# Four adjacent rows of a batch in one partition, and the first rows loaded as two transfers of two tiles

## The chip, the cores and the metric

The kernel runs on one core of a Trainium2 chip. The metric is the device time of one execution in microseconds (us); lower is better. Inputs lie in DRAM (HBM) when it starts and the result must lie there when it ends.

## The reference

A gated block of a Flamingo-like network, all in float32: a LayerNorm, an attention whose keys and values are 512 context rows followed by the 512 rows themselves, and a feed-forward part with the signs of its weights. There are 4 batches of 512 rows and 512 features.

```python
def reference(x, ctx, mask, g_xattn, g_ffn, wq, wk, wv, wo, up_w, down_w, up_scale, down_scale, output_scale):
    n = layernorm(x)                                   # x is (4, 512, 512), rows of 512 features
    q, k_new, v_new = n @ wq.T, n @ wk.T, n @ wv.T
    k, v = concat([ctx, k_new], 1), concat([ctx, v_new], 1)      # 1024 keys
    x = x + tanh(g_xattn) * (softmax(q @ k.T / sqrt(512)) @ v @ wo.T)
    h = relu((layernorm(x) @ sign(up_w).T) * up_scale)            # 2048 hidden
    return x + tanh(g_ffn) * (h @ sign(down_w).T) * down_scale * output_scale
```

Each output row depends on its own input row and, through the softmax, on all rows of its batch in any order: if the rows of a batch are numbered differently inside the kernel, the new keys and values are numbered in the same way, and the result is the same once each row is stored where it belongs.

## The kernel before

All four batches of `x` live in one tile, `rows`, of 128 partitions x 16 tiles x 512 features (a *tile* is here 128 rows of a batch, one in each partition). Tile `r` of a batch holds rows 128r to 128r+127: partition p has row 128r + p (`x_v`, L51, and `out_v`, L54). So the load of one tile reads 256 KB that lie together in DRAM, 2 KB for each partition, and the load of a whole batch reads four pieces of 2 KB for each partition.

Every float32 product is made of three matmuls over a high and a low part (`PASSES`), so each operand goes through ACT (a copy to the high part, rounded) and then DVE or POOL (the low part, the difference). Engines are driven by instruction lists written out by hand, and each waits on semaphores.

*SP* issues all the transfers, in the order of its list (L160 to L211). At the start it issues the first batch's tiles 0 and 1 of `x`, each a transfer with its own semaphore `x0_in[r]` (L170), then the first two quarters of `wk` (L172), then tiles 2 and 3, then the other two quarters of `wk`, then `wq` (L173), the first context (L174), `wo`, `wv`, three gates, two scale vectors and the first signs. A quarter of `wk` is 2 KB out of every 8 KB in DRAM, for `wk` is laid out as `[p, e, c, n]` and quarter `e` is loaded for all p. After that SP waits for POOL's low parts of `wk` (`w_ready`) and loads the whole of batch 1 of `x` (L186) into the place of `wk`'s raw rows, and later batches 2 and 3 (L188, L192) in the same way. At the end it stores the 16 result tiles of 256 KB (L204, and L210 for the last four), each when its rows are ready.

*DVE* starts with `first_stats(0)`, `first_stats(1)`, `first_norm(0)`, `first_norm(1)`, `first_stats(2)`, then the low parts of the turned tiles 0 and 1 (L626), `first_stats(3)`, the low parts of the first two quarters of `wk` (L730), `first_norm(2)` and `first_norm(3)` (L725), and the low parts of turned tiles 2 and 3. `first_stats(r)` waits for `x0_in[r]` (L716) and computes mean and variance (L717, L719, L721); POOL turns variance to the inverse standard deviation (`rstd`, L232) in between. Later batches are normed from L656 on.

*ACT* starts with the high parts of `wk`'s quarters 0 and 1 (L484), the high parts of turned tiles 0 and 1 (L492), `wk`'s quarters 2 and 3, and turned tiles 2 and 3.

*PE* starts with the transposes of normed tiles 0 and 1 (L281, into `turn`), then `first_k_half` (L392), matmuls of 256 columns: for output chunks 0 and 1 of K the pass high x high over the first 256 rows (8 matmuls, which need both turned tiles' high parts), the pass with the low part of the rows (8, which need `turn_lo` at 2), the pass with the low part of `wk` (8, `first_lo`), 16 matmuls for chunks 2 and 3; then the transposes of tiles 2 and 3 (L281, into `proj`), 8 matmuls that need POOL's low parts of `wk` (L237), and 48 for the second 256 rows, which need the turned tiles 2 and 3. From then on PE has Q, the scores, and all the rest (L289, L440, L453).

Of the kernel before, what the change touches and what calls it, by code (L numbers as in the profile page):

```python
# [11 lines left out]
P = 128  # L12
# [4 lines left out]
def gated_block(nc, x, ctx_kv, ctx_turned, g_xattn, g_ffn, wk, wq, wv, wo, ffn_w, up_scale, down_scale,  # L17
# [3 lines left out]
    BATCH, ROWS, DIM = x.shape  # L21
    HC = ffn_w.shape[0]
    RT = ROWS // P
# [24 lines left out]
        return PROJS_FIRST + PROJS_BATCH * b  # L48

    row_tiles = "(r p) d -> p r d"  # L50
    x_v = x.rearrange("b (r p) d -> b p r d", p=P)  # L51
    ctx_v = ctx_kv.rearrange("b (r p) d -> b p r d", p=P)
    ctx_turned_v = ctx_turned.rearrange("b (c p) k -> b p c k", p=P)
    out_v = out.rearrange("b (r p) d -> p (b r) d", p=P)  # L54

    with ExitStack() as stack:
        def sb(name, shape, dt=F32):
            return stack.enter_context(nc.sbuf_tensor(name, shape, dt))
# [4 lines left out]
        def sem(name):  # L63
            return stack.enter_context(nc.semaphore(name))

        rows = sb("rows", [P, BATCH * RT, DIM])
# [49 lines left out]
            return wide(n) if n < DC else proj[:, n % 2, :]  # L116

        small_in, ctx_in, out_stored = map(sem, ("small_in", "ctx_in", "out_stored"))
        x0_in = [sem(f"x0_in{i}") for i in range(RT)]
        x_in = {b: sem(f"x_in{b}") for b in range(1, BATCH)}  # L120
        wk_in = [sem(f"wk_in{i}") for i in range(DC)]
        w_in = {w: sem(f"w_in{w}") for w in (W_Q, W_V, W_O)}
# [18 lines left out]
        LAST = RT * (BATCH - 1)  # L141
# [10 lines left out]
        def turned_split(b):  # L152
            return 2 * b

        def values_split(b):
            return 2 * b + 1
# [3 lines left out]
        @block.sync  # L160
        def _(sp):
            def load_signs(j):
                if j >= 1:
                    sp.wait_ge(signs_ready, j)
                sp.dma_start(raw_w[:, :, :], ffn_w[j]).then_inc(signs_in, 16)


            for half in ((0, 1), (2, 3)):
                for r in half:
                    sp.dma_start(rows[:, r, :], x_v[0, :, r, :]).then_inc(x0_in[r], 16)  # L170
                for e in half:
                    sp.dma_start(raw_of[W_K][:, e, :], wk[:, e].rearrange("p c n -> p (c n)")).then_inc(wk_in[e], 16)  # L172
            sp.dma_start(raw_of[W_Q], wq.rearrange("p e c n -> p e (c n)")).then_inc(w_in[W_Q], 16)  # L173
            sp.dma_start(raw_ctx[:, :, :], ctx_turned_v[0]).then_inc(ctx_in, 16)  # L174
            sp.dma_start(raw_of[W_O], wo.rearrange(row_tiles, p=P)).then_inc(w_in[W_O], 16)
            sp.dma_start(raw_of[W_V], wv.rearrange(row_tiles, p=P)).then_inc(w_in[W_V], 16)
            for i, g in enumerate((g_xattn, g_ffn, output_scale)):
                sp.dma_start(gates_raw[:, i:i + 1], g.rearrange("(a n) -> a n", a=1).broadcast_to([P, 1])
                             ).then_inc(small_in, 16)
            sp.dma_start(out_gain[:, :], down_scale.rearrange("(a n) -> a n", a=1).broadcast_to([P, DIM])  # L180
                         ).then_inc(small_in, 16)
            sp.dma_start(hid_gain[:, :], up_scale).then_inc(small_in, 16)
            load_signs(0)

            sp.wait_ge(w_ready, SPLIT[W_K] + DC - BY_VECTOR)
            sp.dma_start(rows[:, RT:2 * RT, :], x_v[1]).then_inc(x_in[1], 16)  # L186
            sp.wait_ge(w_ready, SPLIT[W_Q] + DC - BY_VECTOR)
            sp.dma_start(rows[:, 2 * RT:3 * RT, :], x_v[2]).then_inc(x_in[2], 16)  # L188
            sp.wait_ge(ctx_ready, turned_split(0) + 1)
            sp.dma_start(raw_ctx[:, :, :], ctx_v[0]).then_inc(ctx_in, 16)  # L190
            sp.wait_ge(w_ready, SPLIT[W_V] + DC - BY_VECTOR)
            sp.dma_start(rows[:, 3 * RT:4 * RT, :], x_v[3]).then_inc(x_in[3], 16)  # L192

            for b in range(1, BATCH):
                sp.wait_ge(ctx_ready, values_split(b - 1) + 1)
                sp.dma_start(raw_ctx[:, :, :], ctx_turned_v[b]).then_inc(ctx_in, 16)
                sp.wait_ge(ctx_ready, turned_split(b) + 1)
                sp.dma_start(raw_ctx[:, :, :], ctx_v[b]).then_inc(ctx_in, 16)

            for j in range(1, HC):  # L200
                load_signs(j)
            for t in range(BATCH * RT - RT):
                sp.wait_ge(out_ready, t + 1)
                sp.dma_start(out_v[:, t, :], rows[:, t, :]).then_inc(out_stored, 16)  # L204
            for r in (0, 2, LAST_POOL, 3):
                if r == LAST_POOL:
                    sp.wait_ge(pool_out_ready, 1)
                else:
                    sp.wait_ge(out_ready, RT * (BATCH - 1) + LAST_DVE.index(r) + 1)
                sp.dma_start(out_v[:, LAST + r, :], rows[:, LAST + r, :]).then_inc(out_stored, 16)  # L210
            sp.wait_ge(out_stored, 16 * BATCH * RT)  # L211

        @block.gpsimd
# [406 lines left out]
        def _(dve):  # L620
# [92 lines left out]
                    proj_out(m + 12 + e, chunk(qT, e), SCALE)  # L713

            def first_stats(r):
                dve.wait_ge(x0_in[r], 16)  # L716
                dve.bn_stats(stats[:, r, :], rows[:, r, :]).then_inc(stats_done, 1)  # L717
                dve.wait_ge(stats_done, r + 1)
                dve.bn_aggr(mean_var[:, r, :], stats[:, r, :]).then_inc(meanvar_done, 1)  # L719
                dve.wait_ge(meanvar_done, r + 1)  # L720
                dve.tensor_scalar(var_eps[:, r:r + 1], mean_var[:, r, 1:2], EPS, None, ALU.add).then_inc(eps_done, 1)  # L721
# [6 lines left out]
            def first_weight_low(e):  # L728
                dve.wait_ge(w_hi, SPLIT[W_K] + e + 1)
                dve.tensor_tensor(weights[:, W_K, LO, e, :], raw_of[W_K][:, e, :],  # L730
                                  weights[:, W_K, HI, e, :].bitcast(F32), ALU.subtract).then_inc(first_lo, 1)

            first_stats(0)
            first_stats(1)
            first_norm(0)
            first_norm(1)
            first_stats(2)
            turn_out(0, part(xT, 0))
            turn_out(1, part(xT, 1))
# [123 lines left out]
```

## Time and profile before

| | us |
|---|---|
| median of 3 runs | 629.65 |
| lowest, highest | 629.64, 630.89 |
| the profiled execution | 629.46 |
| its span in the trace | 627.4 |
| PE busy | 615.0 (98% of the span) |
| DVE, ACT, POOL busy | 247.9, 177.6, 71.1 |
| granted PE clock, mean | 0.999 |

The time of the profiled execution is 2.06 us more than its span: that lies outside of what the trace has. In the trace an instruction is given by its start in us from the span's start, its duration, engine, line, and what it writes and reads; square brackets say how long its engine had been idle before it and who ended that. PEld is the loading of weights into PE, beside the matmuls. SPq is SP's issuing of a transfer, not the transfer; the time from an issue to the landing is given separately. A matmul's own duration overlaps with its neighbours', so a stretch of matmuls is priced by its length over its count.

### The profile page before, as it was taken

How to read it: one execution, taken by the hardware profiler on the slowest of the kernel's cores; microseconds unless marked ns; L12 is line 12 of the kernel's file. 1: busy time of each engine (PE TensorE's matmuls, PEld its weight loads, DVE VectorE, ACT ScalarE, POOL GpSimd, SP SyncE). 2: the span in 40 equal slices, each digit the busy share in tenths (PEclk: the TensorE clock that was granted, in tenths of full speed). 3: DMA queues.
4: the chain of work that ended last, by engine and by line, in shares of the span. 5: the costliest groups of instructions: out<-in, count | busy, mean ns of one | idle time of the engine just before them, and what ended most of it. 6: DMA issues, size and time to landing. Idle time of an engine off the chain costs nothing.

```text
span 627.4 us, 6781 instructions
## 1 busy us (share of the span) xinstructions
PE 615.0 (98%) x2864; PEld 512.5 (82%) x2864; DVE 247.9 (40%) x430; ACT 177.6 (28%) x273; POOL 71.1 (11%) x49
## 2 busy tenths in 40 slices
PE   5999999999999999999999999999999999999997
PEld 5888888888888888888888888888888888888885
DVE  5336322226322226222236223453574366436234
ACT  3624321214221224231236243322212222312211
POOL 3660202000202001202001100100010001000002
PEclk9999999999999999999999999999999999999999
DMA  8740102000101000102013323200010010001001
GB/s 301 282 139 1 68 0 68 0 1 1 67 1 67 1 0 1 68 0 68 0 34 101 100 70 132 68 0 1 18 50 1 0 47 21 1 1 67 2 0 67
DMA packets 13517, 30.05 MB, mean 48 GB/s; under 512 B 1456, under 2 KB 1456, under 8 KB 13360
## 3 DMA queue, kind: packets, MB, share of 16 engines
q1 hardware_dynamic: 13488, 29.64, 13.5%
q8 instruction: 22, 0.36, 0.2%
q14 instruction: 7, 0.06, 0.0%
HBM read 25.44 MB, written 4.19 MB: 47 GB/s over the span
## 4 chain that ended last, share of the span: by engine, by line
PE 96%; ACT 1%; DVE 1%; DMA 1%; SPq 0%; issue 0%; ACTq 0%
PE proj L289 32%; PE score L289 21%; PE proj L440 19%; PE score L453 18%; PE turn L281 4%; PE score L392 2%; DMA rows<-in_wk 1%; ACT four_x L488 0%; DVE rows L812 0%; ACT four_x L492 0%; DVE raw_ctx L809 0%; DVE four_x L626 0%; DVE neg_max L646 0%; ACT probs L500 0%; ACT probsT L492 0%; ACT weights L509 0%
## 5 line engine op out<-in xcount | busy, mean ns | idle before, releaser
L440 PE MATMUL proj<-four_x,weights 128*128 128x512 f32 x512 | 127.6, 392 | 0.0
L453 PE MATMUL score<-weights,probsT 128*128 128x512 f32 x512 | 126.5, 390 | 0.2 <-DVE probsT L769 0.2
L453 PEld LDWEIGHTS score<-weights,probsT 128*128 128x128 f32 x512 | 96.1, 188 | 20.6 <-DVE probsT L769 0.6
L440 PEld LDWEIGHTS proj<-four_x,weights 128*128 128x128 f32 x512 | 95.3, 188 | 19.3
L289 PE MATMUL score<-four_x 128*128 128x512 f32 x384 | 89.9, 392 | 0.0
L289 PE MATMUL proj<-probsT,four_x 128*128 128x512 f32 x384 | 89.9, 392 | 0.0
L599 ACT ACTIVATE probs<-proj,hid_gain 128x512 f32<-128x512 f32 x64 | 43.9, 687 | 147.6 <-PE proj L440 147.6
L496 ACT ACTIVATE four_x<-proj 128x512 fp32r<-128x512 f32 x60 | 35.8, 599 | 172.6 <-PE proj L289 172.6
L289 PEld LDWEIGHTS proj<-probsT,four_x 128*128 128x128 f32 x384 | 71.5, 188 | 14.5
L289 PEld LDWEIGHTS score<-four_x 128*128 128x128 f32 x384 | 71.5, 188 | 14.5
L632 DVE TENSOR_TENSOR four_x<-proj,four_x 128x512 fp32r<-128x512 f32 x44 | 30.3, 691 | 122.1 <-ACT four_x L496 122.1
L289 PE MATMUL proj<-four_x,weights 128*128 128x512 f32 x336 | 76.8, 389 | 0.0
L289 PEld LDWEIGHTS proj<-four_x,weights 128*128 128x128 f32 x336 | 63.0, 188 | 13.0
L767 DVE CAST probsT<-probs 128x512 fp32r<-128x512 f32 x64 | 27.2, 425 | 111.6 <-ACT probs L599 111.6
L242 POOL TENSOR_TENSOR four_x<-raw_ctx,four_x 128x2048 fp32r<-128x2048 f32 x8 | 36.9, 4610 | 122.0 <-ACT four_x L488 122.0
L289 PE MATMUL proj<-weights,four_x 128*128 128x512 f32 x192 | 45.8, 394 | 0.3 <-DVE four_x L632 0.3
L769 DVE TENSOR_TENSOR probsT<-probs,probsT 128x512 fp32r<-128x512 f32 x64 | 44.3, 692 | 2.2
L289 PE MATMUL score<-weights,four_x 128*128 128x512 f32 x192 | 44.2, 389 | 0.0
L289 PEld LDWEIGHTS score<-weights,four_x 128*128 128x128 f32 x192 | 36.1, 188 | 7.5
L289 PEld LDWEIGHTS proj<-weights,four_x 128*128 128x128 f32 x192 | 35.5, 188 | 7.6 <-DVE four_x L632 0.5
L500 ACT ACTIVATE probs<-score,neg_max 128x1024 f32<-128x1024 f32 x16 | 17.9, 1117 | 71.8 <-DVE neg_max L646 71.8
L225 POOL TENSOR_TENSOR var_eps<-mean_var,eps 128x4 f32<-128x4 f32 x7 | 1.7, 237 | 318.4 <-DVE mean_var L661 318.4
(59 smaller groups left out, 367.2 us busy)
## 6 DMA issues: line engine op xcount, KB each, us to landing
raw_w<-in_ffn_w SPq DMA_DIRECT2D x16, 512.0 KB, 3.3
raw_ctx<-in_ctx_turned SPq DMA_DIRECT2D x4, 1024.0 KB, 5.4
raw_ctx<-in_ctx SPq DMA_DIRECT2D x4, 1024.0 KB, 5.2
result<-rows SPq DMA_DIRECT2D x16, 256.0 KB, 2.0
rows<-in_x SPq DMA_DIRECT2D x3, 1024.0 KB, 6.7
rows<-in_x SPq DMA_DIRECT2D x4, 256.0 KB, 4.2
rows<-in_wk SPq DMA_DIRECT2D x4, 256.0 KB, 5.5
rows<-in_wq SPq DMA_DIRECT2D x1, 1024.0 KB, 8.2
```

What stands on the lines that cost most here:

```text
L242: pool.tensor_tensor(ctx_side[:, LO], raw_ctx[:, :, :], ctx_side[:, HI].bitcast(F32), ALU.subtract).then_inc(ctx_ready, 1)
L281: last = pe.transpose(bank[:, k * P:(k + 1) * P], tile, ident[:, :])
L289: last = pe.matmul(bank, lhs(l), rhs(r), start=start and i == 0, stop=stop and i == 2)
L392: last = pe.matmul(proj_bank(e)[:, cut], weights[:, W_K, l, e, c * P:(c + 1) * P], xT[:, r, c, cut], start=i == 0 and c == 0, stop=i == 2 ...
L440: last = pe.matmul(proj[:, j % 2, :], signs[:, j, 0, k * P:(k + 1) * P], four_x[:, c, s, k, :], start=(k == 0 and s == HI), stop=(k == DC ...
L453: last = pe.matmul(wide(r), hid_split[:, j % HR, s, r * P:(r + 1) * P], signs[:, j, 1, :], start=(j == 0 and s == HI), stop=(j == HC - 1 a ...
L496: act.activation(dst, proj_bank(n), ACT.Copy, scale=scale).then_inc(proj_hi, 1)
L500: act.activation(probs[:, t % 2, :], score[t % 2][:, :, :].rearrange("p a n -> p (a n)"), ACT.Exp, bias=neg_max[:, t:t + 1], accum_out=row ...
L599: act.activation(hid[:, j % HR, :], proj[:, j % 2, :], ACT.Relu, scale=hid_gain[:, j:j + 1]).then_inc(relu_done, 1)
L632: dve.tensor_tensor(dst(LO), proj_bank(n), dst(HI).bitcast(F32), ALU.subtract).then_inc(proj_lo, 1)
L767: dve.tensor_copy(slot[:, HI, :], hid[:, j % HR, :]).then_inc(hid_hi, 1)
L769: dve.tensor_tensor(slot[:, LO, :], hid[:, j % HR, :], slot[:, HI, :].bitcast(F32), ALU.subtract).then_inc(hid_ready, 1)
```

## The change

The rows of a batch are dealt out otherwise: partition p holds rows 4p to 4p+3, and tile `r` has row 4p + r in partition p. The view of `x` and that of the result change in the same way, so each row is stored where it came from. A partition's four rows are now 8 KB that lie together in DRAM.

The first batch's rows are loaded by two transfers instead of four: one for tiles 0 and 1, one for tiles 2 and 3, each 4 KB for each partition out of every 8 KB. Each has one semaphore, so there are two `x0_in` instead of four, and `first_stats(r)` waits for `x0_in[r // 2]`. The loads of batches 1 to 3 keep their place and size, but read 8 KB in one piece for each partition instead of four of 2 KB. The 16 stores keep their place, size and semaphores, but write 2 KB out of every 8 KB instead of 256 KB together. No instruction of PE, ACT, DVE or POOL is added, removed or moved.

```diff
     row_tiles = "(r p) d -> p r d"
-    x_v = x.rearrange("b (r p) d -> b p r d", p=P)
+    x_v = x.rearrange("b (p r) d -> b p r d", r=RT)
...
-    out_v = out.rearrange("b (r p) d -> p (b r) d", p=P)
+    out_v = out.rearrange("b (p r) d -> b p r d", r=RT)
...
-        x0_in = [sem(f"x0_in{i}") for i in range(RT)]
+        x0_in = [sem(f"x0_in{i}") for i in range(RT // 2)]
...
             for half in ((0, 1), (2, 3)):
-                for r in half:
-                    sp.dma_start(rows[:, r, :], x_v[0, :, r, :]).then_inc(x0_in[r], 16)
+                sp.dma_start(rows[:, half[0]:half[1] + 1, :], x_v[0, :, half[0]:half[1] + 1, :]
+                             ).then_inc(x0_in[half[0] // 2], 16)
                 for e in half:
                     sp.dma_start(raw_of[W_K][:, e, :], wk[:, e].rearrange("p c n -> p (c n)")).then_inc(wk_in[e], 16)
...
-                sp.dma_start(out_v[:, t, :], rows[:, t, :]).then_inc(out_stored, 16)
+                sp.dma_start(out_v[t // RT, :, t % RT, :], rows[:, t, :]).then_inc(out_stored, 16)
...
-                sp.dma_start(out_v[:, LAST + r, :], rows[:, LAST + r, :]).then_inc(out_stored, 16)
+                sp.dma_start(out_v[BATCH - 1, :, r, :], rows[:, LAST + r, :]).then_inc(out_stored, 16)
...
             def first_stats(r):
-                dve.wait_ge(x0_in[r], 16)
+                dve.wait_ge(x0_in[r // 2], 16)
```

## Rows read from the trace of the kernel before

**Rows 1.** The page: busy time by engine; the transfers of the result.
```profile
PE 615.0 (98%) x2864; PEld 512.5 (82%) x2864; DVE 247.9 (40%) x430; ACT 177.6 (28%) x273; POOL 71.1 (11%) x49
...
result<-rows SPq DMA_DIRECT2D x16, 256.0 KB, 2.0
```
**Rows 2.** Waits of PE: line waited for, us in total, times, longest us.
```profile
PE turn L281 <- DVE normed L725: 6.2, 1, 6.2
PE score L392 <- ACT four_x L492: 0.8, 1, 0.8
PE score L392 <- DVE four_x L626: 0.6, 1, 0.6
```
**Rows 3.** The chain that ended last, 0 to 30 us: start, us, what.
```profile
2.11 5.27 DMA rows<-in_wk
...
8.04 0.98 ACT four_x L492 x2
...
9.06 7.47 PE score L392 x40
...
18.97 6.02 PE score L392 x48
```
**Rows 4.** Timeline of 0 to 22 us: start, duration, engine, line, operation.
```profile
0.74 0.86 SPq L170 DMA_DIRECT2D rows<-in_x  x2
...
3.54 0.70 DVE L717 BATCH_NORM_STATS2 stats<-rows 128x6 f32<-128x512 f32 x1 [3.54 <-DMA rows<-in_x]
...
6.25 2.03 PE L281 MATMUL turn<-ident,normed 128*128 128x128 f32 x8 [6.25 <-DVE normed L725]
6.53 0.63 ACT L484 ACTIVATE weights<-rows 128x512 fp32r<-128x512 f32 x1 [4.51 <-DMA rows<-in_wk]
6.55 0.55 DVE L725 TENSOR_SCALAR normed<-rows,mean_var,rstd 128x512 f32<-128x512 f32 x1 [0.45 <-POOL rstd L232]
...
7.94 1.06 ACT L492 ACTIVATE four_x<-turn 128x512 fp32r<-128x512 f32 x2
8.05 0.69 DVE L717 BATCH_NORM_STATS2 stats<-rows 128x6 f32<-128x512 f32 x1 [0.95 <-DMA rows<-in_x]
...
9.07 1.28 DVE L626 TENSOR_TENSOR four_x<-turn,four_x 128x512 fp32r<-128x512 f32 x2
...
11.27 1.28 DVE L730 TENSOR_TENSOR weights<-rows,weights 128x512 fp32r<-128x512 f32 x2
...
13.63 2.54 POOL L237 TENSOR_TENSOR weights<-rows,weights 128x512 fp32r<-128x512 f32 x2 [1.12 <-DVE normed L725]
...
16.37 0.60 SPq L186 DMA_DIRECT2D rows<-in_x  x1
17.00 1.08 ACT L492 ACTIVATE four_x<-proj 128x512 fp32r<-128x512 f32 x2 [6.34 <-PE proj L281]
17.13 1.01 PEld L392 LDWEIGHTS score<-four_x,weights 128*128 128x128 f32 x8
```
**Rows 5.** Issue to landing: tiles 0 and 1; `wk` quarter 0; tiles 2 and 3.
```profile
DMA to landing us min/median/max: 2.8/2.9/3.0
...
DMA to landing us min/median/max: 4.9/4.9/4.9
...
DMA to landing us min/median/max: 5.4/5.5/5.6
```
**Rows 6.** GB/s in 40 slices of 0.125 us, 0 to 5, then 5 to 10.
```profile
GB/s 0 0 0 0 0 0 0 0 0 0 0 0 0 0 16 115 98 16 131 229 360 410 410 410 377 426 410 410 361 344 295 246 246 197 279 328 262 197 82 49
...
GB/s 49 98 131 213 213 230 229 229 262 279 262 279 344 279 377 393 377 377 393 377 361 410 295 393 311 426 393 426 410 442 492 393 377 426 410 541 475 262 393 524
```
**Rows 7.** Busy time by stretch; after POOL: granted clock, DMA share, GB/s.
```profile
9.00:14.50 5.50, 5.44 (x25) 5.44 (x26) 4.48 (x10) 1.27 (x3) 1.96 (x2) 1.00 1.02 400
```
**Rows 8.** Batch 1: landing of its load (L186), first use.
```profile
DMA to landing us min/median/max: 12.4/12.4/12.4
...
51.02 2.46 DVE L656 BATCH_NORM_STATS2 stats<-rows 128x6 f32<-128x512 f32 x4
```
**Rows 9.** The last two stores: issue to landing.
```profile
DMA to landing us min/median/max: 2.0/2.1/2.1
```

## The prediction, made before the changed kernel was run

> **What bounds the kernel now.** I read the page's busy times first, then the waits of PE, then the chain that ended last, then the timeline of the first 22 us, and last the rates and landings of the transfers. PE is busy for 615.0 of 627.4 us [rows 1]. Of its waits only three matter, and all three lie in the first 19 us: 6.2 us until the first normed tile, 0.8 us for ACT's copies, 0.6 us for DVE's low parts [rows 2]. The rest of the span is a row of matmuls without a gap worth naming, and then a tail of some us with the last sums and stores. So a load that is off the path by many us can't matter, and the change can move the time in two places alone: in what stands ahead of PE's start, and in the last store.
>
> The chain of the start [rows 3] goes by a quarter of `wk` that lands at 7.38, ACT's copies that end at 9.02, and PE's 40 matmuls from 9.06. It doesn't name `x`. The reader must see how near the other branch runs. Tile 0 is issued at 0.74 and DVE starts on it at 3.54; the second normed tile ends at 6.55 + 0.55 = 7.10; PE's eight transposes end at 6.25 + 2.03 = 8.28; ACT's second copy starts at about 7.94 + 1.06 - 0.58 = 8.42 [rows 4]. The branch of `x` has only 8.42 - 8.28 = 0.14 us to spare.
>
> **The change part by part.**
>
> *The first pair.* Before, tile 0 lands 2.8 us after its issue, at 3.54; tile 1, issued 0.43 us later at 1.17, lands 3.0 us after that, at 4.17 [rows 4, 5]. The pair is now one transfer with one semaphore, issued at 0.74, and DVE can't start before all 512 KB are there. The transfers run at 410 GB/s in this stretch [rows 6], so 256 KB more cost 0.64 us: 3.54 + 0.64 = 4.18. Pieces of 4 KB instead of 2 KB may save a little: where `wq` comes in with pieces of 8 KB, from 8.5 us on, the rate has slices of 442 to 541 [rows 6], and at 442 the pair's 512 KB would take 0.09 us less. I take 4.10, so DVE starts 0.56 us later. Below, the bound is 3.9 us (the whole rate of the best slices, and one issue less in front); above, it is the landing of a strided read as in the first rival.
>
> *What that delays.* DVE's chain of the two tiles has no other outside wait than POOL's `rstd`, which moves with it. Its tile 1 was never late for it: it landed at 4.17 and DVE came to it about 1 us after 3.54. So the whole chain shifts by 0.56: the second normed tile ends at 7.66, the transposes at 8.84, ACT's second copy starts at 8.86 instead of 8.42, and PE's first matmul at 9.50 instead of 9.06: 0.44 us later. The two loads of `wk` get their issues 0.45 us earlier, but the bytes ahead of them on the queue are the same, and ACT isn't waiting for them any more.
>
> *What 0.44 us are worth at the end.* Between 9.06 and 14.5 PE makes 25 matmuls in 5.44 us, 0.218 us each [rows 7]; the 48 of the same shape later take 6.02 us, 0.125 each [rows 3]. That is the lower of the clock's two levels (256 columns at 1.2 GHz are 0.213 us), although the view prints a granted clock of 1.00 for the stretch: its record seems not to reach back so far, and the matmuls themselves are the better witness. The 40 matmuls of 7.47 us [rows 3] are then some 26 at the lower and 14 at the upper level, and the rise is near 14.7. If it stays there, a late start takes matmuls out of the slow stretch and puts them in the fast one: 0.44 x 0.125 / 0.218 = 0.25 us. If it moves with the start of the work, all 0.44 us are lost. I take 0.3, near the first, as I see no reason for the rise to move by so little a shift. On this the Trainium skill, page "TensorE: Matmul & The Clock Gate", Part 1, says that the default clock is the throttled one, that activity releases it, and that the point of the rise varies by about 500 ns from run to run because it isn't tied to the kernel's start; by that page the term could be 0.25 us with about 0.2 us either way, an estimate, and no view here can tell it from the other reading.
>
> *The second pair.* Tile 2 lands at 8.05, where DVE is waiting for it, and tile 3 at about 3.07 + 5.6 = 8.67 [rows 4, 5]. Now both land together at about 8.6. The wait stands in `first_stats(2)`; behind it on DVE are the low parts of the turned tiles 0 and 1, which PE's second eight matmuls need. They end at 9.07 + 1.28 = 10.35 now, and at 10.90 then. PE needs them after its first eight: at 9.50 + 8 x 0.218 = 11.24. That leaves 0.34 us where there are 0.45 now. Next: the low parts of `wk`, 11.27 to 12.55 now [rows 4], come 0.55 us later; the first is ready at 12.5 and wanted at 12.98, the second ready at 13.1 and wanted at 13.86. Then `normed` of tiles 2 and 3 and, behind them, POOL's low parts, which end at 13.63 + 2.54 = 16.17 now, 16.72 then; PE wants them at about 17.2 [rows 4] and later. Every one of these is covered, by 0.3 us at the least; if the pair lands later than 8.95 the first cover is gone, and from there on each 0.1 us costs up to 0.1 us. I put it at nothing, with 0 to 0.3 us as bounds.
>
> *The 0.6 us wait at 18.97* is for turned tiles 2 and 3, whose transposes stand behind the 40 matmuls on PE. It moves with them and stays as long as it is.
>
> *The loads of batches 1 to 3.* Batch 1 is issued at 16.37, behind POOL's low parts, and lands 12.4 us later, at 28.8; DVE first reads it at 51.02 [rows 4, 8]. Half a us later, or some tenths of a us shorter through the larger pieces, it is hidden by 22 us. Batches 2 and 3 have a whole batch more. Nothing. What stands behind them on SP's queue (contexts, signs) moves by half a us and is wanted far later.
>
> *The issues.* SP has two issues less of 0.43 us each, 0.86 for two [rows 4]. SP isn't on the path behind the first pair: what it issues then queues for the same engines. Nothing.
>
> *The stores.* Sixteen of 256 KB, 2.0 us each [rows 1]; twelve are covered by matmuls. The last lands about 2.0 us after its issue [rows 9], and that ends the span. It is still 128 pieces of 2 KB, but 8 KB apart in DRAM. No row shows such a write. The nearest are the reads of `wk` with the same spacing: quarters 2 and 3, from 8.2 us on, run in slices of 295 to 492 GB/s, as fast as anything [rows 6]; quarter 0 is slow, and belongs to the rival below. So nothing, with -0.1 to +0.5 us as bounds.
>
> The sum for the profiled execution: 629.46 + 0.3 = 629.76. The median of the runs shown lies 0.19 us above that execution, so the median of the changed kernel should be 629.95 us.
>
> **The rivals.**
>
> *A strided first read is slow (slower).* The first pair reads 4 KB out of every 8 KB over 1 MB, where a tile read 256 KB in one stretch. `wk`'s quarter 0 reads with just this spacing and is the first touch of its tensor: it lands at 1.65 + 4.9 = 6.55, which is 2.38 us after tile 1 for a quarter that is worth 0.64 at 410 GB/s, and the rate falls to 49 GB/s in between [rows 5, 6]. If the pair meets the same 1.7 us, it lands at 5.8, PE starts 2.26 - 0.14 = 2.12 us late, and the loss is 1.2 us (the rise stays) to 2.1 us (it moves): a median of 630.85 to 631.8, say 631.3. Against it speaks that tile 0, also a first touch, started with slices near 16 to 131 GB/s for half a us only, and that quarter 0 may have been slow for its place in time and not for its spacing: quarters 2 and 3 weren't. It decides for "slower" from a landing of the pair at about 5 to 6 us. The Trainium skill, page "DMA: Bandwidth & Descriptors", section "Latency and other measured facts", has a loss of rate for row pitches of 512 KiB and up; with our pitch of 8 KiB it would have this rival at nothing, and that no run here shows yet.
>
> *The clock rises later (slower).* Each us that the lower level lasts longer costs 1 - 0.125 / 0.218 = 0.43 us. The runs of before spread by 1.24 us, which would be a rise 2.9 us later. If the late start pushes the median of the new runs into that case, it is 629.95 + 1.24 = 631.2.
>
> *The start gets faster (below before).* If the larger pieces and the issue saved bring the pair in at 3.7 us and the second pair before 8.05, the shift of the branch is no more than its 0.14 us to spare, and ACT, no more held by a quarter of `wk` that was issued 0.45 us later, starts its copies some tenths earlier. That gives 629.4 to 629.6. For it speaks only the saved issue; against it, that the bytes come at the full rate already.
>
> *The change doesn't do what it says.* If the pair is cut into pieces of 2 KB, it lands at 4.18 and not at 4.10: 0.05 us more. Same result.
>
> **How the numbers follow.** A difference of 0.2% (1.26 us) is about what a measurement of this kernel can tell from none. Forecast (629.7 to 630.3): 0.62. Cut into 2 KB: 0.08, same time. Faster start: 0.09, nearly all of it within 0.2%. Strided first read: 0.14, of which a third stays within 0.2%. Later rise: 0.07. So faster 0.02, same 0.82, slower 0.16. The range from 629.4 to 631.3 leaves out the worse half of the two slow cases and a little below.
>
> **What would show each step.** Right: DVE's first row at about 4.1 with a wait for `in_x`; ACT's first copies waiting for the transposes and no more for `wk`; PE's 40 matmuls from 9.5; no new wait of PE between 9.5 and 17; the last store landing 2.0 us after its issue. Wrong: DVE's first row past 4.9; a wait of PE for L626 or L730 before 14; a PE that starts before 9.06; or a last store that takes over 2.5 us.

## The result, and the profile after

| | before | changed |
|---|---|---|
| median of 22 runs each, us | 629.61 | 631.07 |
| lowest, highest | 628.45, 630.89 | 630.01, 631.61 |
| ratio of the times, 95% interval | | 1.0020 (1.0014 to 1.0026) |
| the profiled execution | 629.46 | 631.44 |
| its span | 627.4 | 629.4 |

The change makes the kernel 1.46 us slower by the medians, 1.26 us (0.9 to 1.6) by the ratio: just at the bound of 0.2% that the prediction had set for a difference. The profiled executions are 1.98 us apart, more than the medians: what follows explains the two executions first, and only then the medians.

The page of the changed kernel, the lines that answer to [rows 1]; the busy times are the same, the stores are not:

```profile
PE 614.9 (98%) x2864; PEld 512.3 (81%) x2864; DVE 248.0 (39%) x430; ACT 177.6 (28%) x273; POOL 71.2 (11%) x49
...
result<-rows SPq DMA_DIRECT2D x16, 256.0 KB, 2.5
```

The waits of PE in the changed kernel, to be held against [rows 2]:

```profile
PE turn L281 <- DVE normed L725: 7.7, 1, 7.7
PE score L392 <- ACT four_x L492: 0.7, 1, 0.7
PE score L392 <- DVE four_x L626: 0.6, 1, 0.6
PE proj L289 <- DVE four_x L632: 0.3, 1, 0.3
PE score L453 <- DVE probsT L769: 0.2, 1, 0.2
```

The first wait has grown from 6.2 to 7.7 us; the others are within 0.1 us of what they were. The chain that ended last, 0 to 30 us (start, us, what):

```profile
0.74 4.22 DMA rows<-in_x
4.96 0.02 issue
4.99 0.70 DVE stats L717
...
7.09 0.47 DVE normed L725
7.55 0.14 issue
7.69 2.04 PE turn L281 x8
9.72 0.02 issue
9.75 0.61 ACT four_x L492
10.35 0.04 issue
10.40 7.47 PE score L392 x40
...
20.32 6.02 PE score L392 x48
```

In [rows 3] this chain went by `in_wk`. Now it goes by the pair of `in_x`, which lands 4.22 us after its issue, at 4.96, and DVE starts at 4.99 instead of 3.54. PE's 40 matmuls start at 10.40 instead of 9.06 and take 7.47 us in both executions; the 48 that follow start at 20.32 instead of 18.97. So 1.35 us of the 1.98 are in place by 20 us, and nothing more comes until the tail: DVE's last row, first before, then in the changed kernel, is again 1.34 us apart.

```profile
623.84 1.00 DVE rows L812
```
```profile
625.18 1.00 DVE rows L812
```

Both rows start 607.31 us after the end of the 40 matmuls (16.53 and 17.87). In 13 of the 14 profiled executions of this study that stretch is 607.3 to 607.4 us; so the time of an execution is decided by when its 40 matmuls end, and by its last store.

The stores and the two `x` pairs in the changed kernel (issue to landing: all 16 stores; the last store; the first pair; the second pair):

```profile
DMA to landing us min/median/max: 2.4/2.5/2.8
...
DMA to landing us min/median/max: 2.8/2.8/2.8
...
DMA to landing us min/median/max: 4.2/4.2/4.2
...
DMA to landing us min/median/max: 7.1/7.1/7.1
```

A store was 2.0 us [rows 1], the last one 2.1 [rows 9]. The last store is issued at 624.87 and lands at 627.01 before, 626.21 and 628.99 in the changed kernel: 2.14 and 2.78 us. The 0.64 us between them are the rest of the 1.98.

What in a store is longer can be read from the rate of the transfers in the 2 us after one lone store is issued (40 slices of 0.05 us; first before, from 621.38, then changed, from 622.72):

```profile
GB/s 0 0 0 0 0 0 0 0 0 0 0 0 0 0 0 0 246 164 451 287 451 451 246 532 287 410 492 246 532 205 164 82 0 0 0 0 0 0 0 0
```
```profile
GB/s 0 0 0 0 0 0 0 0 0 0 0 0 0 0 0 0 246 164 451 492 246 492 287 451 451 287 451 328 451 287 123 41 0 0 0 0 0 0 0 0
```

Both begin 0.8 us after the issue and are over at 1.6. The DMA engines move the bytes in the same time. Only the landing is told later: 2.0 us after the issue in one kernel, 2.5 in the other.

### The profile page after: what moved, and what is told of

It reads as the page before. It is cut to its first block, busy times and chain, and to the rows that moved or that the text cites. A ratio compares the mean times of both kernels' runs of the same rounds, so it can differ in the third digit from the quotient of the medians.

```text
span 629.4 us, 6779 instructions
## 1 busy us (share of the span) xinstructions
PE 614.9 (98%) x2864; PEld 512.3 (81%) x2864; DVE 248.0 (39%) x430; ACT 177.6 (28%) x273; POOL 71.2 (11%) x49
## 4 chain that ended last, share of the span: by engine, by line
PE 96%; DVE 2%; ACT 1%; DMA 1%; issue 0%; ACTq 0%
PE proj L289 32%; PE score L289 21%; PE proj L440 19%; PE score L453 18%; PE turn L281 4%; PE score L392 2%; DMA rows<-in_x 1%; ACT four_x L488 0%; DVE rows L812 0%; DVE raw_ctx L809 0%; DVE stats L717 0%; DVE four_x L626 0%; DVE neg_max L646 0%; ACT four_x L492 0%; ACT probs L500 0%; ACT probsT L492 0%
```

## The experiments

After the result one theory stood against three rivals. The theory: the spacing of 8 KB costs at both ends, in the first read and in what follows the last byte of a store, and the merge of two tiles adds its own 0.6 us. The rivals: all the loss is at the start; or the size of one transfer matters and not its spacing; or the slow stretch in the first us has its place in time, whatever is read.

### The stores alone

> The kernel before with the stores of the change alone (2 KB out of every 8 KB); the loads are as before, so the rows of a batch come out in another order. Theory (the strided write is confirmed later): each store lands 2.4 to 2.5 us after its issue instead of 2.0, the last one 2.7 to 2.8 instead of 2.1, the start is as before (PE's 40 matmuls from 9.06), and the time is 0.5 to 0.7 us over the kernel before, 630.1 to 630.3 at its median of 629.6. Rival (the stores of the changed kernel were slow only because of where its end fell): landings of 2.0 and 2.1, and the time of before within 0.1 us.

```diff
-    out_v = out.rearrange("b (r p) d -> p (b r) d", p=P)
+    out_v = out.rearrange("b (p r) d -> b p r d", r=RT)
...
-                sp.dma_start(out_v[:, t, :], rows[:, t, :]).then_inc(out_stored, 16)
+                sp.dma_start(out_v[t // RT, :, t % RT, :], rows[:, t, :]).then_inc(out_stored, 16)
```

Measured: ratio 1.0012 (1.0003 to 1.0020), medians 630.08 and 629.65. The stores land after 2.4 to 2.5 us and the last after 2.77. The store part is shown: it needs nothing of the new loads. (This one profiled execution has 0.45 us more in its middle, 607.75 us from the end of the 40 matmuls to DVE's last row; no other has that, and the 11 runs' median doesn't rest on it.) The start wasn't what I expected, though the loads are those of before:

```profile
2.10 6.04 DMA rows<-in_wk
...
9.82 7.24 PE score L392 x40
```

`wk`'s quarter 1 lands at 8.14 and not at 7.38, and PE starts 0.76 us later than in [rows 3]. This turned out to matter more than the run's own question; see the repeats below.

### The loads alone

> The changed kernel with the stores of before; the rows of a batch come out in another order. Theory (start and end add up): DVE starts near 5.0, PE's 40 matmuls near 10.4, stores land after 2.0 and 2.1 us, and the time is 0.7 to 1.0 us over the kernel before, so that with the stores alone it makes the 1.46 us of the change. Rival (all of the loss is at the start): 1.3 to 1.5 us over the kernel before.

The edit is the change without its two lines of stores. Measured: ratio 1.0012 (1.0004 to 1.0021), medians 630.36 and 629.65. The pair lands 4.1 us after its issue, DVE starts at 4.88, which is 1.46 us after the 3.42 of the run of the stores alone, PE's 40 matmuls at 10.29; the stores take 2.0 us, the last 2.15. The loads alone cost 0.7 us by either measure, the stores alone 0.4 by the medians and 0.8 by the ratio; together that is 1.1 to 1.5 us, and the change has 1.46 and 1.26. "All at the start" falls by the store's landing and by the run of the stores alone; this run's own interval, 0.25 to 1.3 us, only just excludes it.

```profile
4.88 0.71 DVE stats L717
```

### The merge without the spacing

> The kernel before, rows placed as before, with the first rows in two transfers of two tiles, each 512 KB in one stretch: the merge without the stride. Batch 3 of x, far from any other work, is loaded tile by tile with a semaphore each. Theory (two causes at the start): the pair lands near 4.1, as the prediction had it, PE's 40 matmuls start near 9.5, and the time is 0.2 to 0.45 us over the kernel before; the four tiles of batch 3 land one after another, the first after at most 3 us. Rival (the size of one transfer is the cause, not its spacing): the pair lands near 5.0 here too and PE starts near 10.4.

```diff
-        x0_in = [sem(f"x0_in{i}") for i in range(RT)]
+        x0_in = [sem(f"x0_in{i}") for i in range(RT // 2)]
...
-                for r in half:
-                    sp.dma_start(rows[:, r, :], x_v[0, :, r, :]).then_inc(x0_in[r], 16)
+                sp.dma_start(rows[:, half[0]:half[1] + 1, :], x_v[0, :, half[0]:half[1] + 1, :]
+                             ).then_inc(x0_in[half[0] // 2], 16)
...
-            sp.dma_start(rows[:, 3 * RT:4 * RT, :], x_v[3]).then_inc(x_in[3], 16)
+            for r in range(RT):
+                sp.dma_start(rows[:, 3 * RT + r, :], x_v[3, :, r, :]).then_inc(x3_in[r], 16)
```

Measured:

```profile
4.17 0.71 DVE stats L720
```

PE's 40 matmuls start at 9.58 and take 7.27 us; the time is 629.82 against 629.65, ratio 1.0004 (0.9996 to 1.0013), which doesn't tell it from no change. At DVE the merge alone is +0.63 us over the 3.54 of [rows 4], and +0.75 over the 3.42 of the run of the stores alone, which was measured beside it and has the loads of before. The prediction had worked out 0.56 to 0.64 from the rate.

### The spacing without the merge

> Rows placed as in the changed kernel, but the first rows in four transfers of one tile, each 2 KB out of every 8 KB: the stride without the merge; stores as before, so the rows of a batch come out in another order. Batch 3 is loaded tile by tile as in the run of the merge alone, here with the stride. Theory (a first read with gaps is slow): tile 0 lands 0.4 us or more later than at 3.54, near 4.0 to 4.9, and the first tile of batch 3 lands 0.3 us or more later after its issue than in the run of the merge alone, its second, third and fourth not. Rival (a slow stretch at a fixed place in time, 4.5 to 6.5 us, whatever is read): tile 0 lands at 3.54 as before, batch 3's first tile takes what it takes without the stride, and the time is that of before within 0.15 us.

```diff
-    x_v = x.rearrange("b (r p) d -> b p r d", p=P)
+    x_v = x.rearrange("b (p r) d -> b p r d", r=RT)
```

and batch 3 by tiles as above. DVE starts on tile 0 at 4.37:

```profile
4.37 0.71 DVE stats L720
```

That is 0.83 us later than 3.54, and 0.95 later than the 3.42 measured beside it, for the same 256 KB in the same place in time, because its pieces lie 8 KB apart. With the merge that makes 1.46 or 1.70, and the changed kernel has 4.99 - 3.54 = 1.45. So both causes are needed and together they cover what the start of DVE shows; that one of the sums meets it to 0.01 us is luck, as tile 0's landing varies by 0.35 us (below). The total again can't be told from no change: ratio 1.0004 (0.9995 to 1.0013).

Batch 3 gives the same read far from any other work. The landing of its first tile, first in one stretch (the merge run), then with the spacing:

```profile
DMA to landing us min/median/max: 2.5/2.5/2.5
```
```profile
DMA to landing us min/median/max: 3.2/3.2/3.2
```

0.7 us, from one execution each. The whole batch differs less: issues and landings of the four tiles span 41.3 to 46.6 in one, 40.5 to 46.2 in the other, 5.3 and 5.7 us. The tiles in one stretch go slower one by one (2.5, 3.3, 3.8 and 4.0 us), with the spacing the first tile takes most of it (3.2, 3.6, 4.1 and 4.3). So the second, third and fourth tiles are later too, by 0.3 us each, where I had expected nothing for them. Why the first tile takes most of it isn't shown, nor whether it has to be a first read: no run reads the same rows a second time. The rival of a slow place in time falls: the cost follows the spacing to 41 us.

### `wk` in stretches

> The kernel before with another host layout of wk, [e, p, c, n] instead of [p, e, c, n]: each quarter is 256 KB in one stretch, not 2 KB out of every 8 KB. Theory (a first read with gaps is what is slow): quarter 0 lands 1 us or more earlier than 4.9 to 5.0 after its issue, quarter 1 at least 0.5 us earlier, the chain of the start no more goes by wk, PE's 40 matmuls start at 8.8 to 9.0 whatever the draw, and the time is 0.1 to 0.5 us under the kernel before. Rival (quarter 0 is slow for its place in time): its landing stays within 0.3 us and so does the time.

```diff
-                    sp.dma_start(raw_of[W_K][:, e, :], wk[:, e].rearrange("p c n -> p (c n)")).then_inc(wk_in[e], 16)
+                    sp.dma_start(raw_of[W_K][:, e, :], wk[e].rearrange("p c n -> p (c n)")).then_inc(wk_in[e], 16)
...
-        'wk': by_columns(given('L0_xattn_wk')),
+        'wk': _np.ascontiguousarray(by_columns(given('L0_xattn_wk')).transpose(1, 0, 2, 3)),
```

Measured: quarter 0 lands 3.9 us after its issue and not 4.9 [rows 5], quarter 1 after 4.1. The chain now goes by tile 0 of `x`:

```profile
3.38 0.70 DVE stats L717
...
8.80 6.30 PE score L392 x40
```

Median 628.74 against 629.35, ratio 0.9992 (0.9983 to 1.0001), which by itself doesn't quite tell it from no change. I ran it again beside another run, below.

### Half the spacing, and twice the spacing, for the stores

> The kernel before with stores of half the gap: each tile writes 2 KB out of every 4 KB over 512 KB, instead of 256 KB in one stretch or 2 KB out of every 8 KB over 1 MB; rows come out in another order. Theory (the landing is confirmed later the wider the stretch is that a store writes over): its stores land 2.1 to 2.4 us after the issue, between the 2.0 and the 2.5 of the two others. Rival (any gap costs the same): 2.5. Rival (only the 8 KB spacing costs): 2.0.

```diff
-    out_v = out.rearrange("b (r p) d -> p (b r) d", p=P)
+    out_v = out.rearrange("b (h p r) d -> b h p r d", h=2, r=2)
```

> The kernel before with stores of twice the gap of the change: each tile writes 2 KB out of every 16 KB over 2 MB; rows come out in another order. Stores took 2.0 us at 2 and 4 KB from piece to piece, 2.5 at 8 KB. Theory (the confirmation is later from a spacing of 8 KB on, growing with it): 2.6 to 3.2 us. Rival (one step that all spacings of 8 KB and more share): 2.4 to 2.5 us. Rival (8 KB is a special spacing): 2.0.

```diff
-    out_v = out.rearrange("b (r p) d -> p (b r) d", p=P)
+    out_v = out.rearrange("b n d -> (b n) d").rearrange("(g p r) d -> g p r d", g=2, r=2 * RT)
```

Measured: with 4 KB from piece to piece a store takes 2.0 us and the last 2.14; with 16 KB it takes 2.0 and the last 2.13. The last two stores of the 16 KB run:

```profile
DMA to landing us min/median/max: 2.0/2.1/2.1
```

Each of the two was executed once; what is read from them is the stores. My theory of a growing price fell twice. The spacings of 2 KB (one stretch), 4 and 16 KB are all alike, and only 8 KB is late. Across all profiled executions the last store takes 2.13 to 2.16 us in the ten without the 8 KB spacing and 2.77 or 2.78 in the four with it. Why 8 KB, these runs don't say. The width that a store writes over (1 MB) was the other thought; the 16 KB run writes over 2 MB and excludes a price that grows with width.

### Both kernels once more

> The kernel before once more, for the spread of its start from one execution to the next. Theory (the first transfers and the rise of the clock vary from execution to execution by some tenths of a us to 2 us, apart from the change): the landing of wk's quarter 1 and the length of the 40 matmuls differ from 7.38 and 7.47 us by over 0.2 us in one of the two, while tile 0 lands within 0.15 us of 3.54. Rival: all is repeated within 0.1 us.

> The changed kernel once more. Theory: the pair lands within 0.15 us of 4.96 and the stores take 2.4 to 2.5 us again, the last 2.7 to 2.8, since these come from the addresses; the 40 matmuls may have another length than 7.47, between 5.5 and 8, since the rise of the clock has its own time. Rival: the pair's landing varies as widely as wk's, by 0.5 us or more.

The same kernel before, another execution:

```profile
2.11 6.62 DMA rows<-in_wk
...
10.41 6.48 PE score L392 x40
```

The same changed kernel, another execution:

```profile
4.64 0.70 DVE stats L717
...
10.06 6.46 PE score L392 x40
```

DVE started at 3.19 and 4.64 here, not 3.54 and 4.99: both 0.35 us earlier, so both guesses of "within 0.15 us" were too tight, while the difference of 1.45 us stands. The stores are as they were, 2.13 and 2.77 at the end. The two executions took 629.85 and 630.07 us, only 0.22 apart: the changed one's 40 matmuls ended 0.37 us before the other's, and its last store took 0.64 more. What matters is `wk`: its quarter 1 landed at 8.73, and PE of the kernel *before* started at 10.41, as late as that of the changed one. The table has every profiled execution whose first loads are those of before or those of the change; all but the last have `wk` as it was:

| execution | DVE starts | PE's 40 matmuls start | take | `wk` quarter 1 lands |
|---|---|---|---|---|
| before | 3.54 | 9.06 | 7.47 | 7.38 |
| before, again | 3.19 | 10.41 | 6.48 | 8.73 |
| stores alone | 3.42 | 9.82 | 7.24 | 8.14 |
| stores at 4 KB | 3.21 | 10.57 | 7.68 | 8.89 |
| stores at 16 KB | 3.49 | 8.90 | 7.64 | 7.12 |
| changed | 4.99 | 10.40 | 7.47 | |
| changed, again | 4.64 | 10.06 | 6.46 | |
| loads alone | 4.88 | 10.29 | 7.03 | |
| changed, `wk` in stretches (below) | 5.41 | 10.82 | 7.41 | |

With the loads of before the start is 9.75 us in the mean and varies by 1.7. With those of the change it is 10.25 and varies by 0.3; with the last row, 10.39 and 0.8. The profile that the prediction rested on had one of the two earliest starts of five, and the latest tile 0. The executions come from several chips, so what varies from chip to chip and what from execution to execution isn't told apart.

### `wk` in stretches, in both kernels

> The changed kernel with wk laid out so that each quarter is one stretch of 256 KB. In the kernel before this layout took PE's 40 matmuls from a start of 9.1 to 10.6 us to 8.80. Theory (the pair of x, not wk, holds the start of the changed kernel): wk lands earlier but PE still starts at 9.9 to 10.5, and the time stays within 0.4 us of the changed kernel, 1.2 to 1.6 us over the kernel before. Rival (the slow wk makes both slow): PE starts before 9.6 and the time falls by 0.5 us or more.

> The kernel before with the layout of wk alone, once more, beside the run of the changed kernel with that layout. Theory: quarter 1 lands near 6.2 again, PE starts at 8.7 to 9.0, stores take 2.0 us, and the time is 0.3 to 0.9 us under the kernel before. Rival (the first run had a lucky draw of the clock): PE's start varies by over 0.5 us from the first run's 8.80, or the time is within 0.2 us of the kernel before.

Both have the edit of `wk` shown above. Measured for the changed kernel: 631.15 us, ratio to the kernel before 1.0024 (1.0015 to 1.0034); `wk` lands earlier (quarter 1 at 1.6 + 5.2 = 6.8), and PE waits for the pair as ever, though a little later than I had expected (9.9 to 10.5):

```profile
5.41 0.70 DVE stats L717
...
10.82 7.41 PE score L392 x40
```

For the kernel before: 628.74 us again, against 629.54, ratio 0.9988 (0.9980 to 0.9997), PE from 8.75. So `wk` in stretches is worth 0.6 to 0.8 us to the kernel before (by the medians; the second run's interval is 0.2 to 1.3 us) and nothing that shows to the changed one. What the change costs depends on what it is laid beside: 1.46 us while the slow `wk` covers part of it, 631.15 - 628.74 = 2.4 us when that cover is gone. In this execution the pair took 4.6 us instead of 4.2, so the pair's landing varies too, 4.6 to 5.4 at DVE in four executions.

### Two rows to a partition

> The change with two adjacent rows to a partition instead of four, over half a batch (loads of a pair are one stretch of 512 KB, stores write 2 KB out of every 4 KB), and wk laid out in quarters of one stretch. Theory (the change's losses are the 8 KB spacing at both ends plus the merge): stores take 2.0 us, the pair lands at 3.9 to 4.2, PE's 40 matmuls start at 9.3 to 9.5, 0.6 us after the 8.80 of the kernel before with that wk, and the time is 0.2 to 0.6 us over that kernel's: 629.0 to 629.3 beside a kernel before of 629.55. Rival (the merge costs as much as the spacing): PE starts at 10 or later, the time is over that of the kernel before.

```diff
-    x_v = x.rearrange("b (p r) d -> b p r d", r=RT)
+    x_v = x.rearrange("b (h p r) d -> b p h r d", h=2, r=2)
...
-    out_v = out.rearrange("b (p r) d -> b p r d", r=RT)
+    out_v = out.rearrange("b (h p r) d -> b h p r d", h=2, r=2)
```

Measured: the pair lands at 4.2, the 40 matmuls start at 9.62, a tenth of a us later than expected, stores take 2.0 us, the last 2.15; 629.35 us against 629.36, ratio 1.0002 (0.9993 to 1.0011). Without the 8 KB spacing the store's loss is gone, and DVE starts at 4.21 instead of 4.64 to 5.41. What is left is the merge, 0.6 us over the kernel before with that `wk` (629.35 against 628.74, of different sessions), at the upper end of what I expected. The merge gains nothing in either form that was run. The fastest kernel of this study is the kernel before with `wk` in stretches.

## Why the prediction was right, and where it was off

The time, 631.07, lies in the range (629.4 to 631.3), and its sign, slower, was that of the sum. But the likeliest value was 629.95, and the loss is 1.46 us where the sum had 0.3. The time misses even the forecast's own band (629.7 to 630.3); it is inside the range because the range had been stretched for the rivals. And two of the signs that the prediction had named for a wrong step appeared: DVE's first row came past 4.9 (4.99), and the last store took over 2.5 us (2.78). Point by point:

*Which two places can matter* (what stands ahead of PE's start, and the last store): right. PE's other waits changed by no more than a tenth of a us, and the 607.3 us behind the 40 matmuls are the same in both kernels.

*The first pair*: off. I took a landing at 4.10, from the rate; it was 4.96. The merge was priced about right, as its own run shows (4.17 at DVE). What failed is that the first rival, the slow first read with gaps, was given a chance instead of a share in the sum. The mechanism was named and the price bounded at 1.7 us by the nearest row, `wk`'s quarter 0; it came out at 0.8 to 1.0 us at DVE. I had set it at zero because tile 0 wasn't slow, but tile 0 was read in one stretch and says nothing on gaps. The Trainium skill, page "DMA: Bandwidth & Descriptors", section "Latency and other measured facts", lists a loss for row pitches from 512 KiB up. It has no figure for smaller ones, so the prediction went beyond it in reading "nothing" there; here a pitch of 8 KB costs 0.7 to 1.0 us in a first read, and the measurement decides.

*The 0.14 us to spare*: the step that failed most, though it hardly shows in the total. I took the landing of `wk` in one execution, 7.38, as that of the kernel. It goes from 7.12 to 8.89, and in three of five executions it is later by 0.76 us or more. In every execution whose chain goes by `x`, PE starts 5.41 or 5.42 us after DVE; so in the five with the loads of before the branch of `x` had 0.1, 1.8, 1.0, 1.95 and 0.0 us to spare, 1.0 in the mean. DVE starts 1.6 us later in the mean of the four executions with the changed loads, and PE's 40 matmuls 0.64 (10.39 against 9.75), not the 1.33 that the two first traces make believe. The prediction had 0.44. That this is near is luck: it had DVE's delay too small by 1.05 us (0.56 against 1.61) and the spare time too small by 0.8, and the errors went against each other.

*What a late start is worth*: priced too low, as far as the traces can tell. I had taken 0.3 of 0.44 us, near the case in which the clock's rise stays where it is. The 40 matmuls take 6.29 to 7.68 us; at 0.218 and 0.125 us per matmul that is 15 matmuls more or less at the lower level, a slow stretch 3.3 us longer or shorter, and it puts the rise between 11.9 and 16.9 us of the span. If the rise stayed, they would take 0.43 us less for each us that they start later. Over the 14 profiled executions their length shows no such fall: the straight line that fits them best has +0.13 us for each us, with a standard error of 0.22. So on average the case "it moves with the start of the work" fits, and the case "it stays" fits badly; what sets the rise in a single execution isn't shown, and it scatters the time by 1.4 us, beside a spread of 2.4 us over the runs of the kernel before. On this the Trainium skill's page "TensorE: Matmul & The Clock Gate", Part 1, holds that the rise isn't tied to the kernel's start, and the traces agree, with a spread far wider than the 500 ns it gives. So the scatter that the rival "clock rises later" lived on is under both kernels, whatever the change does. In time, the loss by the ratio without the last store's 0.64 is 1.26 - 0.64 = 0.62 us (0.2 to 1.0), and the loads' own run has 0.76 (0.25 to 1.3). Both are near the whole of the 0.64 us at PE's start, but the intervals hold the lower price (0.57 x 0.64 = 0.36) as well.

*The second pair, the weights, the issues, the later batches*: right, nothing. The second pair landed at 9.2, past the 8.95 that the prediction had named as the limit, but PE was later by then too: DVE's wait for it is 0.69 us, PE has no wait in its 40 matmuls, and POOL's low parts end at 17.34 with PE at them from 18.50.

*The stores*: the term was mis-sized. I set nothing, with +0.5 as the bound, from the rate at which `wk`'s later quarters were read. The rate was indeed the same; but what grew is the time between the last byte and the landing, and no read row shows that. It is +0.6 us on the last store in every execution, and 0.43 to 0.76 us in the time of its own run (by the medians and by the ratio).

*The chances*: "within 0.2%" had 0.82, and the time came out at the very bound of it, 0.23% by the medians and 0.20% by the ratio. The 0.16 on slower was too little. Two unknown costs that could hardly be gains were both put at zero.

## What to carry to other kernels

When a change merges two loads whose first part is awaited, it trades the first part's early landing for one issue less, and the issue wasn't on the path; here that cost DVE 0.6 to 0.8 us and gained nothing. When a layout changes the spacing of a transfer on the path, price it from a transfer with that spacing and in the same role (first touch or not, read or write), and give an unknown that can only be a loss a share of its bound in the sum, not a rival's chance. And a margin of 0.14 us read from one execution is no margin: take a second trace before building on which of two branches is the later.

## What the runs showed of the hardware

- A store of 128 pieces of 2 KB lands 0.4 to 0.5 us later when the pieces lie 8 KB apart in DRAM (2.5 us instead of 2.0; the last one, beside another, 2.78 instead of 2.14), with the bytes moved in the same time. At 2, 4 and 16 KB apart it doesn't.
- A first read of 256 KB as 2 KB out of every 8 KB lands later than one stretch: by 0.8 to 1.0 us when issued at 0.7 us of the span, by 0.7 at 41 (one execution each); three further tiles out of the same 1 MB were then 0.3 us late.
- The landing of `wk`'s quarter 1, an early load with gaps, varies by 1.8 us between five executions with the same first loads (7.12 to 8.89), that of tile 0 in one stretch by 0.35 (DVE's start at 3.19 to 3.54). The executions are of several chips.
- The time at which PE's clock rises scatters: 40 equal matmuls took from 6.29 to 7.68 us, and their length didn't fall with a later start. The granted clock printed for these stretches was 1.00 throughout, so the matmuls' spacing (0.218 us before the rise, 0.125 after it) must be read instead.
